# Keys spread two tiles ahead on GpSimd, and mask matmuls ahead of score matmuls

## The chip, the cores and the metric

The kernel runs on one core of a Trainium2 chip. Time is device time of the whole execution in microseconds (us), lower is better. Engines are named as in the profile: PE is TensorE's matmuls and PEld its weight loads, DVE is VectorE, ACT is ScalarE, POOL is GpSimd, SP is SyncE, which issues the DMAs.

## The reference, cut to what matters

There are 32 batches of a context `ctx` (128 channels by 1024 positions). Two things are computed from it and combined. The first is attention within chunks of 64 positions, with 8 heads of 16 channels and one bias for masked keys:

```
scores = einsum('bnqhd,bnkhd->bnhqk', qh, kh) * scale
scores = scores + where(mask > 0, 0.0, -1e9)
out    = softmax(scores) @ v, projected, masked, plus x, then normalised over positions
```

The second is a nearest-neighbour search over each batch: pairwise distances of all 1024 positions, the 30 nearest of each position (`top_k(pd, 30)`), the differences of three coordinates to each neighbour, their length and two angles. Those go through batch norms, give weights, and the weighted sum of neighbours is added to the first part.

## The kernel before, in words

`stage_a` (lines 146 to 1160) does attention, the distances, the top 30, the gathering of the neighbours' coordinates and the angles. Stage B (about 4140 to 4340 us) sums batch-norm moments, stage E (to the end) applies the weights. Only stage A is touched.

A batch `b` has 8 tiles of 128 positions (`TILES`), in two halves of 4 (`QT`). Each engine has its own program, an instruction stream with waits on semaphores, and each runs the batches through `emit(b, j, par, first, last)`: four batches written out, a loop over pairs of batches, and two written out. Order within an engine is fixed by that program.

DVE takes the tiles in pairs (0,1), (2,3), (4,5), (6,7). For a pair it does four rounds `r` of MAX8, FIND_INDEX8 and (but for the last) MATCH_REPLACE8 on 1024 distances per row (lines 866 to 873). Behind rounds 0 and 2 it takes the reciprocal of a tile's softmax sums (`inverse`, L900) and the row maxima of a tile's scores (`largest`, L896). Behind round 2 of pair (2,3) and of pair (6,7) it splits the found indices of half a batch into digits (`digits`, L827, L831, L835). Behind round 1 of pair (6,7) it takes the reciprocal of the denominators of the angles of batch `b-2` (`denoms`, L891), which waits for POOL's `sph_denoms` of that batch.

PE, iteration `t`: units of the gather for batch `b-1` (a one-hot fill L482 and 12 short matmuls L503), the two halves of the distances of tile `t+2` (L407, L409, bank `pd_ps`), then `scores` of tile `t+1`, a unit, the transposes `turn_probs` of tile `t-1` (L453), a unit, `values` of tile `t-1` (L463), and by the iteration further projections (L568, L425, L416). The scores of a tile are one PSUM bank `s_ps` of 128 x 512: partitions 0 to 63 are the tile's first chunk (`e` = 0), partitions 64 to 127 its second. Each chunk's half is a bf16 mask matmul from 32 rows (L441), which starts the accumulation, and an f32 matmul of 128 rows (L444), which ends it. `scores` waits until ACT has taken the exponents of the tile before from the same bank (`exp_ready`), and until POOL has written this tile's keys (`kz_ready`).

ACT, iteration `t`: it empties the one-hot banks (L588 to `ohT`), the distance halves (L588 to `pd_sb`), takes the exponents of tile `t` between the two distance halves (L754), then empties what PE made.

POOL, iteration `t` (lines 1032 to 1087): `spread_keys` (L1115) multiplies the tile's keys with the head mask into `kz[:, t % 2]`, two buffers of 128 x 1024 f32, and waits until the scores two tiles before have been made. Behind it stands `normalise` of tile `t-1` (L1091), which waits for DVE's `inverse` and releases PE's `turn_probs`. Then come parts of the gather for the batch before (L958 to L965), and in some iterations long pieces: at `t` = 3 `sph_signs` of batch `b-2` (16 steps, L987 to L1003), at `t` = 4 `invert` and `squares_split` (L916 to L929), at `t` = 5 `sph_denoms` (L1011 to L1015).

Keys and queries of a half lie in `kt` and `qs`. PE makes those of the next half at the end of iterations 2 and 6 and ACT writes them; ACT's write of `kt` waits until all four tiles of the old half have been spread.

Of the kernel before, what the change touches and what calls it, by code (L numbers as in the profile page):

```python
# [25 lines left out]
HEADS, CHUNK = 8, 64  # L26
# [7 lines left out]
QT = TILES // QUADS  # L34
# [111 lines left out]
def stage_a(nc, x, ctx, mask, w_in, b_in, w_out, b_out, consts, y_dram, cst, con, planes, idx_all, stats_all):  # L146
    OHR = 3
    XR = 97
    with ExitStack() as st:
        def sb(name, shape, dt=F32):  # L150
            return st.enter_context(nc.sbuf_tensor(name, shape, dt))
# [40 lines left out]
        qs = sb("qs", [P, HALF])  # L192
        kt = sb("kt", [P, HALF])
        kz = sb("kz", [P, 2, 2, HEADS, CHUNK])
# [11 lines left out]
        s_ps = st.enter_context(nc.psum_tensor("s_ps", [P, HEADS, CHUNK], F32))  # L206
# [72 lines left out]
        def misc_base(b):  # L279

            return 5 if isinstance(b, int) and b == 0 else b * FILLS
# [8 lines left out]
        def batches(eng, emit):  # L290

            emit(0, 0, 0, True, False)
            emit(1, 0, 1, False, False)
            emit(2, 1, 0, False, False)
            emit(3, 1, 1, False, False)
            with eng.Fori(2, B // 2 - 1) as j:
                emit(j * 2, j, 0, False, False)
                emit(j * 2 + 1, j, 1, False, False)
            emit(B - 2, B // 2 - 1, 0, False, False)
            emit(B - 1, B // 2 - 1, 1, False, True)  # L300
# [60 lines left out]
        def _(pe):  # L361
            pe.wait_ge(w_in_landed, 96)
            for g in range(4):
                m = nc.tensor.transpose(mi_ps[0][:, g * C:(g + 1) * C], wnat[:, g, :], con["ident"])
# [64 lines left out]
            def scores(b, par, t):  # L429

                s = b * TILES + t

                if not (isinstance(s, int) and s == 0):
                    pe.wait_ge(exp_ready, s)
                pe.wait_ge(kz_ready, s + 1)
                if t == 0:
                    pe.wait_ge(minv_ready, b + 1)
                for e in range(2):
                    ch = 2 * (t % QT) + e
                    keys = minv[:, par, (2 * t + e) * CHUNK:(2 * t + e + 1) * CHUNK]  # L440
                    nc.tensor.matmul(s_ps[64 * e:64 * e + 64], negs[MASKS],  # L441
                                     keys.rearrange("p (o k) -> p o k", o=1).to_broadcast([32, HEADS, CHUNK]),
                                     start=True, stop=False)
                    m = nc.tensor.matmul(s_ps[64 * e:64 * e + 64], qs[:, bass.ts(ch, CHUNK)], kz[:, t % 2, e],  # L444
                                         start=False, stop=True)
                m.then_inc(s_ready, 1)

# [462 lines left out]
        def _(pool):  # L910
# [121 lines left out]
            def emit(b, j, par, first, last):  # L1032
                second = isinstance(b, int) and b == 1
                steps = Steps((b - 1) * GSTEPS - (0 if first or second else len(slot_groups[0]) * 4))
                for t in range(TILES):
                    h = t // QT
                    s = b * TILES + t

                    if t % QT != QT - 1:
                        spread_keys(b, t + 1)  # L1040

                    if t == QT - 1:
                        pool.wait_ge(misc_moved, misc_base(b) + (8 if first else 12))
                        spread_keys(b, t + 1)
                    elif t == TILES - 1 and not last:
                        pool.wait_ge(misc_moved, misc_base(b) + (24 if first else 29))
                        spread_keys(b + 1, 0)
                    if t > 0 or not first:
                        normalise(s - 1, (t - 1) % TILES)
                    if t == QT + 1:  # L1050
                        rows(b, j, par, 0, misc_base(b) + (15 if first else 20))
                    elif t == 1 and not first:
                        rows(b - 1, (b - 1) // 2 if isinstance(b, int) else (j - 1 if par == 0 else j), 1 - par, 1, misc_base(b) + 4)
                    if t == 0 and not first:
                        keep(b - 1, 1 - par)
                    if t == 3 and not first:
                        convert(b - 1, 1)
                    if t == 7:
                        convert(b, 0)
                    if t > 0 and not first:  # L1060
                        gather(b - 1, 1 - par, 0 if t <= QT else 1, slot_groups[t % QT], steps)
                    elif t == 0 and not first and not second:
                        gather(b - 2, par, QUADS - 1, slot_groups[0], steps)
                    if t == 0 and there(b - 3):
                        sph_ratios(b - 3)
                    if t == 3:
                        if there(b - 3):
                            sph_turn(b - 3)
                        if there(b - 2):
                            sph_signs(b - 2)  # L1070
                    if t == 5 and there(b - 2):
                        sph_denoms(b - 2)
                    if t == 2:
                        split(b, j, par)
                    if t == 1 and not last:
                        square(b + 1, (b + 1) // 2 if isinstance(b, int) else (j if par == 0 else j + 1), 1 - par)
                    if t == 4 and not last:
                        if first:
                            gate(pool, probs_ready, s, pool_gates)
                        else:  # L1080
                            gate(pool, g_done, (b - 1) * NG + GROUPS, pool_gates)
                        invert(b + 1, (b + 1) // 2 if isinstance(b, int) else (j if par == 0 else j + 1), 1 - par)
                        squares_split(b + 1, 1 - par, misc_base(b) + (12 if first else 16))
                    if t == 5 and not first:
                        gate(pool, mv_ready, b, pool_gates)
                        nc.gpsimd.tensor_copy(stats_all[:, bass.ds(b - 1, 1), :].rearrange("p b s -> p (b s)"),
                                              mv[:]).then_inc(mv_kept, 1)

            def normalise(s, t):
                pool.wait_ge(rcp_ready, s + 1)  # L1090
                nc.gpsimd.tensor_tensor(sS[:, t % 2], sS[:, t % 2],  # L1091
                                        rs[:, t % 2, :].rearrange("p (h o) -> p h o", o=1).to_broadcast([P, HEADS, CHUNK]),
                                        ALU.mult).then_inc(probs_ready, 1)

            def rows(b, j, par, h, moved):

                pool.wait_ge(misc_moved, moved)
                if h == 0:
                    pool.wait_ge(mask_landed[par], (j + 1) * 16)
                    pool.wait_ge(x_landed, b * 16 + 16)  # L1100
                cols = bass.ts(h, HALF)
                nc.gpsimd.tensor_tensor(y_s[:, h, :], y_s[:, h, :], maskb[:, par, cols], ALU.mult).then_inc(masked_y, 1)
                pool.wait_ge(masked_y, b * 2 + h + 1)
                nc.gpsimd.tensor_tensor(y_s[:, h, :], y_s[:, h, :], x_s[:, cols], ALU.add).then_inc(y_ready, 1)

            def spread_keys(b, t):

                s = b * TILES + t

                if not (isinstance(s, int) and s < 2):  # L1110
                    pool.wait_ge(s_ready, s - 1)
                c = t % QT
                src = kt[:, 2 * c * CHUNK:2 * (c + 1) * CHUNK].rearrange("p (e o k) -> p e o k", e=2, o=1)
                heads = con["headmask"].rearrange("p (o h u) -> p o h u", o=1, u=1)
                nc.gpsimd.tensor_tensor(kz[:, t % 2], src.to_broadcast([P, 2, HEADS, CHUNK]),  # L1115
                                        heads.to_broadcast([P, 2, HEADS, CHUNK]), ALU.mult).then_inc(kz_ready, 1)
# [12 lines left out]
            def keep(b, par):  # L1129

                gate(pool, topk_done, (b + 1) * TILES, pool_gates)
                for q in range(QUADS):
                    dst = idx_all[:, bass.ds(b * BCOLS + q * QCOLS, QCOLS)].rearrange("p (k t) -> p k t", t=QT)
                    nc.gpsimd.tensor_copy(dst, idx16[:, par, q * QT:(q + 1) * QT, 0:K].rearrange("p t k -> p k t")).then_inc(idx_kept, 1)
# [4 lines left out]
            squares_split(0, 0, 2)  # L1139
            pool.wait_ge(misc_moved, 5)  # L1140
            spread_keys(0, 0)
            batches(pool, emit)
            normalise(B * TILES - 1, TILES - 1)
            rows(B - 1, B // 2 - 1, 1, 1, TAIL + 3)
# [874 lines left out]
```

## Time and profile before

| | |
|---|---|
| median of 3 runs | 5825.07 us (5822.19 to 5827.9) |
| the profiled execution's own time | 5831.42 us |
| its span | 5829.4 us |
| PE busy, share of the span | 4784.7 us, 82% |
| DVE busy | 5153.9 us, 88% |
| ACT busy | 4027.0 us, 69% |
| POOL busy | 3047.6 us, 52% |
| mean granted TensorE clock | 0.908 |

Stage A ends near 4140 us of the span. A batch takes about 126 us there. A busy share over the whole span mixes the stages; POOL works only in stage A. Distances between starts on PE tell more than its busy times, since its matmuls are pipelined.

### The profile page before, as it was taken

What the parts mean: (1) busy time and instruction counts of PE and PEld (TensorE: products, weight loads), DVE (VectorE), ACT (ScalarE), POOL (GpSimd) and SP (SyncE); (2) the same over time, 40 slices, a digit from 0 to 9 for tenths busy, and PEclk for the clock granted to TensorE, in tenths of its full rate; (3) what the DMA queues carried; (4) which work ended last, traced back from release to release, by engine and by line L of the source; (5) the groups of instructions that cost most, each with busy time, mean ns of one, the idle gap of its engine ahead of it and who ended that gap; (6) DMA issues with size and microseconds to landing.
All of it is one profiled execution on the core that took longest, in us unless ns stands there. A gap on an engine that the chain in (4) does not pass through costs nothing. (4 is left out here: it accounts for less than half of the span.)

```text
span 5829.4 us, 169462 instructions
## 1 busy us (share of the span) xinstructions
PE 4784.7 (82%) x63182; PEld 2694.6 (46%) x63182; DVE 5153.9 (88%) x7549; ACT 4027.0 (69%) x9505; POOL 3047.6 (52%) x3780
## 2 busy tenths in 40 slices
PE   6888878888888888888888888887395889899999
PEld 2444444444444444444444444443242666666666
DVE  7999989999999999998999999898298988888887
ACT  3777777777777777777777777776533766666666
POOL 3577777777777777777777777776400000000000
PEclk8999999899898999989999998898697899999999
DMA  0010000010000001000000100000000000000000
GB/s 29 16 31 16 16 17 16 17 31 17 17 16 17 17 16 31 16 17 16 17 17 16 31 16 17 16 16 12 1 0 4 26 27 30 32 26 30 26 30 26
DMA packets 135798, 114.60 MB, mean 20 GB/s; under 512 B 105344, under 2 KB 106112, under 8 KB 134784
## 3 DMA queue, kind: packets, MB, share of 16 engines
q1 hardware_dynamic: 134912, 102.73, 6.0%
q8 instruction: 563, 9.22, 0.7%
q14 instruction: 323, 2.65, 0.2%
HBM read 69.16 MB, written 33.55 MB: 18 GB/s over the span
## 5 line engine op out<-in xcount | busy, mean ns | idle before, releaser
L588 ACT ACTIVATE ohT<-oh_ps 128x512 bf16<-128x512 f32 x1920 | 1149.0, 613 | 564.8 <-PE oh_ps L482 560.4
L866 DVE MAX8 vals<-pd_sb 128x8 f32<-128x1024 f32 x1024 | 1201.0, 1210 | 310.8 <-ACT pd_sb L588 293.4
L871 DVE FIND_INDEX8 idx<-vals,pd_sb 128x8 uint16<-128x1024 f32 x1024 | 1243.6, 1217 | 0.0
L503 PEld LDWEIGHTS g_ps<-tparts,ohT 128*128 128x128 bf16 x23040 | 851.5, 97 | 347.5 <-issue 103.1
L482 PE MATMUL oh_ps<-bitsT,code 128*128 128x512 bf16 x1920 | 777.8, 411 | 284.9 <-ACT bitsT L772 154.0
L873 DVE MATCH_REPLACE8 pd_sb<-vals,pd_sb 128x1024 f32<-128x1024 f32 x768 | 927.5, 1208 | 0.0
L503 PE MATMUL g_ps<-tparts,ohT 128*128 128x24 bf16 x23040 | 869.3, 174 | 3.3
L1955 PEld LDWEIGHTS e_a_ps<-planes,e_oh 120*128 120x128 bf16 x24576 | 687.2, 97 | 301.9 <-issue 220.7
L1725 ACT COPY e_at<-e_a_ps 128x512 f32<-128x512 f32 x512 | 543.0, 1061 | 358.5 <-PE e_a_ps L1955 353.6
L1955 PE MATMUL e_a_ps<-planes,e_oh 120*128 120x32 bf16 x24576 | 702.1, 178 | 87.6 <-DVE e_oh L1883 46.8
L407 PE MATMUL pd_ps<-ctx_s 128*128 128x512 f32 x1024 | 661.7, 732 | 75.4 <-ACT pd_sb L588 73.6
L444 PE MATMUL s_ps<-kz,qs 128*64 128x512 f32 x1024 | 639.5, 710 | 0.0
L754 ACT ACTIVATE sS<-s_ps,mx 128x64 f32<-128x64 f32 x2048 | 610.7, 329 | 29.8 <-DVE mx L896 28.5
L1883 DVE TENSOR_TENSOR e_oh<-e_pairs,e_iotan 120x2048 bf16<-120x2048 bf16 x512 | 622.2, 1216 | 5.0 <-PE e_a_ps L1955 2.2
L1115 POOL TENSOR_TENSOR kz<-kt,cst 128x1024 f32<-128x1024 f32 x256 | 490.0, 1914 | 242.3 <-ACT kt L588 185.1
L961 POOL TENSOR_TENSOR gsb<-gsb 128x240 f32<-128x240 f32 (+2 forms) x1152 | 544.6, 473 | 90.3
L482 PEld LDWEIGHTS oh_ps<-bitsT,code 128*128 128x128 bf16 x1920 | 187.8, 101 | 850.7 <-issue 443.6
L1969 PE MATMUL e_o_ps<-e_at,e_xT 128*128 128x512 f32 x1024 | 566.6, 648 | 0.2 <-ACT e_at L1725 0.2
L588 ACT ACTIVATE pd_sb<-pd_ps,nxx 128x512 f32<-128x512 f32 x512 | 366.5, 716 | 200.4 <-PE pd_ps L409 200.4
L1091 POOL TENSOR_TENSOR sS<-sS,rs 128x512 f32<-128x512 f32 x256 | 273.2, 1067 | 402.2 <-DVE rs L900 402.1
L754 ACT ACTIVATION_READ_ACCUMULATOR sS<-s_ps,mx 128x1 f32 x2048 | 455.7, 223 | 0.0
L441 PE MATMUL s_ps<-xp,negs 32*64 32x512 bf16 x512 | 221.0, 432 | 278.0 <-ACT sS L754 157.1
(241 smaller groups left out, 7430.5 us busy)
## 6 DMA issues: line engine op xcount, KB each, us to landing
ctx_s<-in_ctx SPq DMA_DIRECT2D x32, 512.0 KB, 4.4
maskb<-in_mask_Bx1x_ff SPq DMA_DIRECT2D x32, 512.0 KB, 6.6
x_s<-in_x SPq DMA_DIRECT2D x32, 512.0 KB, 5.1
y_spill<-y_s SPq DMA_DIRECT2D x32, 512.0 KB, 3.0
e_y<-y_spill SPq DMA_DIRECT2D x32, 512.0 KB, 3.9
out<-e_o SPq DMA_DIRECT2D x64, 256.0 KB, 2.2
table<-in_ctx SPq DMA_DIRECT2D x96, 4.0 KB, 5.8
pd_sb<-in_shape_constants SPq DMA_DIRECT2D x1, 1180.0 KB, 5.3
```

Source lines behind the costliest of these rows:

```text
L407: nc.tensor.matmul(pd_ps[:], ctx_s[:, par, bass.ts(t, P)], ctx_s[:, par, bass.ts(h, HALF)], start=True, stop=False)
L444: m = nc.tensor.matmul(s_ps[64 * e:64 * e + 64], qs[:, bass.ts(ch, CHUNK)], kz[:, t % 2, e], start=False, stop=True)
L482: nc.tensor.matmul(oh_ps[k % 2][:], code[:, k % KT, :], bitsT[:, k // KT, :], start=True, stop=True).then_inc(oh_ready, 1)
L503: m = nc.tensor.matmul(found_ps[gi % 2][:, k % GK, t, :], ohT[:, k % OHR, bass.ts(t, P)], tparts[:, par, part, :], start=(part == 0), stop ...
L588: return nc.scalar.activation(dst, src, func, scale=scale, bias=bias)
L754: m = nc.scalar.activation(sS[:, t % 2, hd, :], s_ps[:, hd, :], ACT.Exp, bias=mx[:, t % 2, hd:hd + 1], accum_out=rs[:, t % 2, hd:hd + 1])
L866: nc.vector.max(vals[:, i, :], pd_sb[:, (t + i) % RING, :]).then_inc(topk_step, 1)
L871: found = nc.vector.max_index(idx16[:, par, t + i, 8 * r:8 * r + 8], vals[:, i, :], work)
L873: nc.vector.match_replace(work, vals[:, i, :], work, REMOVED).then_inc(topk_step, 1)
L1883: v.tensor_tensor(oh[pp, g % RING], low.to_broadcast([QCOLS, NB // 2, LO, 2]), row.to_broadcast([QCOLS, NB // 2, LO, 2]), ALU.is_equal).th ...
L1955: m = nc.tensor.matmul(a_ps[g % 2][:, i].rearrange("p t e -> p (t e)"), oh[pp, g % RING, i // 2, :, i % 2], spr[q][pp, part, :, (g * NB + ...
L1969: m = nc.tensor.matmul(o_ps[q][:], xT[:, par, e, :], at[:, q, e].rearrange("p t n -> p (t n)"), start=(e == 0), stop=(e == HI - 1))
```

## The change

In `scores`, both mask matmuls of a tile are issued first and both score matmuls after them. In POOL's program the keys of tile `t+2` are spread in iterations 0, 1 of each half, none in iteration 2, and those of the next half's first two tiles together in iteration 3. One more spread stands ahead of the first batch. The number of matmuls and of spreads and their operands stay as they were. `spread_keys` itself is unchanged: its wait for the scores two tiles before the spread one stays.

```diff
@@ scores (PE) @@
                 for e in range(2):
-                    ch = 2 * (t % QT) + e
                     keys = minv[:, par, (2 * t + e) * CHUNK:(2 * t + e + 1) * CHUNK]
                     nc.tensor.matmul(s_ps[64 * e:64 * e + 64], negs[MASKS],
                                      keys.rearrange("p (o k) -> p o k", o=1).to_broadcast([32, HEADS, CHUNK]),
                                      start=True, stop=False)
-                    m = nc.tensor.matmul(s_ps[64 * e:64 * e + 64], qs[:, bass.ts(ch, CHUNK)], kz[:, t % 2, e],
+                for e in range(2):
+                    m = nc.tensor.matmul(s_ps[64 * e:64 * e + 64], qs[:, bass.ts(2 * (t % QT) + e, CHUNK)], kz[:, t % 2, e],
                                          start=False, stop=True)
                 m.then_inc(s_ready, 1)
@@ emit (POOL) @@
-                    if t % QT != QT - 1:
-                        spread_keys(b, t + 1)
-
-                    if t == QT - 1:
+                    if t % QT < 2:
+                        spread_keys(b, t + 2)
+                    elif t == QT - 1:
                         pool.wait_ge(misc_moved, misc_base(b) + (8 if first else 12))
                         spread_keys(b, t + 1)
+                        spread_keys(b, t + 2)
                     elif t == TILES - 1 and not last:
                         pool.wait_ge(misc_moved, misc_base(b) + (24 if first else 29))
                         spread_keys(b + 1, 0)
+                        spread_keys(b + 1, 1)
                     if t > 0 or not first:
                         normalise(s - 1, (t - 1) % TILES)
@@ ahead of the batches (POOL) @@
             spread_keys(0, 0)
+            spread_keys(0, 1)
             batches(pool, emit)
```

## Rows read from the trace of the kernel before

**Rows 1.** Waits, whole span: engine line waited for, us in total, times, longest.

```profile
ACT ohT L588 <- PE oh_ps L482: 560.4, 350, 6.2
DVE vals L866 <- ACT pd_sb L588: 293.4, 45, 21.7
```

**Rows 2.** Timeline of DVE in one batch: start, duration, then line, operation, idle before.

```profile
1960.98 1.12 DVE L827 TENSOR_TENSOR bits<-idx,bitval 128x896 uint16<-128x896 uint16 x1
...
2004.42 1.23 DVE L866 MAX8 vals<-pd_sb 128x8 f32<-128x1024 f32 x1 [7.51 <-ACT pd_sb L588]
...
2018.20 1.64 DVE L891 RECIPROCAL rel<-rel 128x240 f32<-128x240 f32 x1
...
2068.28 1.23 DVE L866 MAX8 vals<-pd_sb 128x8 f32<-128x1024 f32 x1 [4.69 <-ACT pd_sb L588]
```

**Rows 3.** Timeline of POOL from iteration 3 to iteration 5 of that batch.

```profile
1957.23 1.90 POOL L1115 TENSOR_TENSOR kz<-kt,cst 128x1024 f32<-128x1024 f32 x1 [2.50 <-ACT kt L588]
1960.59 1.04 POOL L1091 TENSOR_TENSOR sS<-sS,rs 128x512 f32<-128x512 f32 x1 [1.46 <-DVE rs L900]
...
1983.68 1.90 POOL L1115 TENSOR_TENSOR kz<-kt,cst 128x1024 f32<-128x1024 f32 x1 [0.25 <-POOL turn L1003]
1985.54 1.04 POOL L1091 TENSOR_TENSOR sS<-sS,rs 128x512 f32<-128x512 f32 x1
...
2005.37 1.04 POOL L1091 TENSOR_TENSOR sS<-sS,rs 128x512 f32<-128x512 f32 x1
...
2015.74 0.69 POOL L1015 TENSOR_TENSOR rel<-rel 128x240 f32<-128x240 f32 x1 [0.19 <-POOL planes L1014]
```

**Rows 4.** Timeline of PE, iterations 4 and 5 of that batch.

```profile
1985.72 0.37 PE L441 MATMUL s_ps<-xp,negs 32*64 32x512 bf16 x1 [2.42 <-POOL kz L1115]
...
1988.89 0.64 PE L453 MATMUL mi_ps<-cst,sS 128*128 128x128 f32 x4
...
2005.56 0.60 PE L441 MATMUL s_ps<-xp,negs 32*64 32x512 bf16 x1 [4.24 <-POOL kz L1115]
...
2011.22 1.09 PE L453 MATMUL mi_ps<-cst,sS 128*128 128x128 f32 x4
```

**Rows 5.** Windows (length, busy by engine, PEclk): the second of those score blocks.

```profile
2005.60:2010.50 4.90, 4.90 (x7) 0.80 (x8) 4.90 (x10) 0.00 (x0) 4.74 (x5) 0.50 0.00 0
```

**Rows 6.** Timeline of PE: a score block, and a block of 64-column f32 matmuls.

```profile
2052.93 0.40 PE L441 MATMUL s_ps<-xp,negs 32*64 32x512 bf16 x1 [0.52 <-ACT sS L754]
2053.26 1.07 PE L444 MATMUL s_ps<-kz,qs 128*64 128x512 f32 x2
...
2055.59 0.39 PE L482 MATMUL oh_ps<-bitsT,code 128*128 128x512 bf16 x1
...
2059.70 1.97 PE L425 MATMUL mi_ps<-wT,ctx_s 128*64 128x128 f32 x32
2061.61 0.39 PE L482 MATMUL oh_ps<-bitsT,code 128*128 128x512 bf16 x1
```

**Rows 7.** Timeline of POOL and DVE: last denominators of the first and last steady batch.

```profile
375.10 0.71 POOL L1015 TENSOR_TENSOR rel<-rel 128x240 f32<-128x240 f32 x1 [0.18 <-POOL planes L1014]
...
377.95 1.65 DVE L891 RECIPROCAL rel<-rel 128x240 f32<-128x240 f32 x1
...
3916.39 0.71 POOL L1015 TENSOR_TENSOR rel<-rel 128x240 f32<-128x240 f32 x1 [0.18 <-POOL planes L1014]
...
3920.37 1.64 DVE L891 RECIPROCAL rel<-rel 128x240 f32<-128x240 f32 x1
```

**Rows 8.** Timeline of DVE: the digits of pair (6,7) in two batches.

```profile
2027.39 0.61 DVE L827 TENSOR_TENSOR bits<-idx,bitval 128x896 uint16<-128x896 uint16 x1
...
2028.26 0.66 DVE L835 TENSOR_TENSOR hi1h<-hi,hival 128x960 bf16<-128x960 uint16 x1
...
2155.86 2.25 DVE L827 TENSOR_TENSOR bits<-idx,bitval 128x896 uint16<-128x896 uint16 x1
...
2159.20 1.26 DVE L835 TENSOR_TENSOR hi1h<-hi,hival 128x960 bf16<-128x960 uint16 x1
```

## The prediction

> **What bounds the kernel now.** The page's shares come first: DVE is busy 88% of the span, POOL half of it, and POOL works only in stage A. The view by waits then says what DVE lacks there: one line, 293.4 us in 45 waits for distances that ACT writes [rows 1]. DVE's timeline shows where. The wait recurs once in each batch, at MAX8 of tile 7 (7.51 us at 2004.42; 7.5 to 10.0 in others), and eight times more at tile 3 (from 923.0 to 3335.99 us, 17.7 us together, the largest 4.69) [rows 2]. Outside these, DVE is busy. So stage A is DVE's work plus some 8 us a batch, and the question is what makes tile 7 late.
>
> Backward from 2004.42: ACT writes tile 7's second distance half behind the exponents of tile 5, those stand behind roots and projections of iteration 4, these behind PE's transposes L453 at 1988.89, these behind the scores of tile 5, which began at 1985.72 after 2.42 us of waiting for `kz` [rows 4]. POOL wrote that `kz` only at 1983.68, behind `sph_signs` [rows 3]. [...]
>
> **The change, part by part.**
>
> Spreads. Tile 5 is now spread in iteration 3, before `sph_signs`, and tile 6 at the start of iteration 4, so both waits of PE for `kz` go. What is late next is `normalise`: in iteration 4 POOL still does one spread (tile 6) behind `sph_signs`, then `normalise(3)`, ending at 1985.54 + 1.04 = 1986.58. PE's transposes can start then instead of at 1988.89: 2.3 us gained [rows 3, 4]. In the same way iteration 5's transposes move from 2011.22 to 2005.37 + 1.04 = 2006.41, 4.8 us earlier [rows 3, 4].
>
> Does the second spread in iteration 3 delay POOL? It adds 1.90 us behind 1957.23 + 1.90; `normalise(2)` began at 1960.59 only after 1.46 us of waiting for DVE, so its start would move from 1960.59 to about 1961.0, and POOL waits for DVE's digits behind it anyway [rows 3]. Cost: nothing while keys come no later than now, up to 1.9 us a batch if they came just in time. They come earlier, see next. The new spread's wait (scores of tile 3) is long met, and the extra buffer it fills is free for the same reason.
>
> Matmul order. A score block takes 2055.59 - 2052.93 = 2.66 us, of which each f32 score takes about 1.0 (2.66 / 2 - 0.33) [rows 6]. Grouped, the two scores stand side by side, in different column halves. No row shows that pair. The nearest is L425: 32 passes of 128 x 128, alternating between column halves, in 2061.61 - 2059.70 = 1.91 us. [...] Bounds: nothing gained (2.66), both wholly side by side (1.3). I take 1.75, by the L425 row. Where it counts: ACT waits after each block for the next fill (560.4 us in 350 waits, 1.6 each), so 0.9 us a tile comes off the PE-ACT chain [rows 1]. Over iterations 0 to 3 that brings keys, and PE's arrival at iteration 4, some 3 us earlier, which covers the spread above.
>
> [...]
>
> What then binds. DVE's gain is not 8 us a batch. DVE's L891 in pair (6,7) waits for POOL's L1015. Here L1015 ended at 2015.74 + 0.69 = 2016.43, and L891 started at 2018.20: 1.77 us later [rows 2, 3]. Between DVE's digits (1960.98) and L1015 POOL runs almost without a gap, 55.5 us, and none of that work is removed or moved off. So the stretch can shrink by this slack alone. The 29 steady pairs, from 375.81/377.95 to 3917.10/3920.37, have slacks of 1.56 to 4.37, sum 69 us [rows 7]. The large ones are batches where PE came late to iteration 4, which the 0.9 per tile mends. Less 0.1 each for the semaphore: 66 us. Where PE now waits for `normalise(3)` for over 2 us its clock can fall to the lower level (as in rows 5); L453 took 1.09 there against 0.64 [rows 4]. I take 1.5 us of that on a third of the batches beyond what the chain's spare 0.6 hides: 8 us lost. 58 us stay.
>
> Tile 3's waits (17.7 us) go with the 4.8 us of iteration 5 [rows 2]. The start and last batches give about 5 more.
>
> Against it: in iteration 7 two spreads in a row meet DVE's digits of pair (6,7). These took from 2028.26 + 0.66 - 2027.39 = 1.53 us with POOL idle to 2159.20 + 1.26 - 2155.86 = 4.60 beside one spread and `normalise` [rows 8]; over the batches they average 3.5. DVE and POOL are now both locked to L1015's end: POOL reaches the pair of spreads about 7.9 us after it, DVE the digits 9.3 after it, so every batch collides, at about 4.6. That is 1.1 x 29 = 32 us lost; bounds from 1.53 (a gain of 57) to one whole spread more, 4.60 + 1.90 (87 lost). [...]
>
> Sum: 58 + 18 + 5 - 32 = 49 us off the profiled execution's 5831.4: 5782. It lies 6.4 above the median of runs, so the median would be 5776.
>
> **Rivals.**
>
> A: the score halves don't overlap. The waits for `kz` still go: PE's arrival in iteration 4 gains 1.3 us in the half of batches that waited for `kz`, the others nothing. About 20 + 18 + 3 - 32 = 9 us: 5816. [...] Chance 0.12.
>
> B: the collision in iteration 7 costs nothing more than now (keys or normalise fall elsewhere) and the clock holds: 66 + 18 + 5 = 89 us less, 5736, or some between. For it: the 1.53 row; against: both engines hang on L1015. Chance 0.15.
>
> [...] Chance 0.08.
>
> D: the change moves waits only, POOL comes later by the second spread (up to 1.9 x 29 = 55 us, eating the 49): 5830, no change. Chance 0.07.
>
> **How the numbers follow.** The forecast's case has 0.58, giving 5776, own range 5755 to 5800. The whole range, 5740 to 5818, takes in most of A and B. A measurement here tells 0.2% (12 us) from no change: faster means under 5813. Faster: 0.58 + 0.15 and a third of A, 0.78 rounded. Same: the rest of A and half of D, 0.12. Slower: C and part of D, 0.10.
>
> **What would show it.** In the profile after: L441's waits for POOL `kz`, as in rows 4, near nothing; start of the mask pair to the next fill 1.75 us at full clock; L453 of iteration 4 directly behind `normalise`; tile 7's wait down to 5 to 6 us; L891 starting within 0.2 us of L1015's end, at times waiting for it; tile 3's waits gone; digits of pair (6,7) near 4.6 in each batch. It is wrong if the block stays above 2.3 us, if L891 keeps its slack, or if tile 7's wait is gone altogether.

## The result, and the profile after

The changed kernel takes 5790.46 us (median of 5 runs, 5786.69 to 5792.12). The kernel before, on the same chip, takes 5822.19 (5 runs, 5817.2 to 5827.9). The ratio is 0.9939, with a 95% interval of [0.9927, 0.9951]: faster by 0.6%. The forecast was 5776, its own range 5755 to 5800. The profiled execution took 5790.79 against 5831.42 before, 40.6 us less; the prediction's sum said 49.

The page of the kernel after, its head, its busy row, and TensorE's granted clock in 40 slices:

```profile
span 5788.7 us, 168877 instructions
...
PE 4476.3 (77%) x62610; PEld 2718.6 (47%) x63182; DVE 5127.8 (89%) x7549; ACT 4035.6 (70%) x9505; POOL 3045.6 (53%) x3780
...
PEclk7888888888888898888888888887697899999999
```

DVE is still the engine that is nearly always busy, and its busy time fell by 26.1 us (5153.9 before) though it runs the same 7549 instructions. The waits of the kernel after (engine line waited for: total us, times, longest), against [rows 1] and the waits for `kz` in [rows 4]:

```profile
DVE vals L866 <- ACT pd_sb L588: 284.0, 35, 21.7
...
ACT ohT L588 <- PE oh_ps L482: 114.4, 245, 2.2
...
DVE rel L891 <- POOL rel L1015: 92.1, 2, 48.5
...
ACT gsb L669 <- POOL planes L965: 86.2, 88, 1.5
...
ACT sS L754 <- DVE mx L896: 168.1, 90, 5.2
...
PE mi_ps L453 <- POOL sS L1092: 66.4, 36, 5.4
```

PE now waits for `kz` only once, 2.8 us ahead of the first scores, and ACT's wait for PE's code planes fell from 560.4 to 114.4 (all idle time ahead of these copies: from 564.8 to 155.3; the trace lacks 572 of the 1920 records of L482 and so cannot name the cause of each wait). Both are what the change aims at, and almost none of it reached DVE: its wait for distances fell by 9.4 only. Two rows are new. ACT now waits 86.2 us in 88 places for POOL's L965, and PE's transposes wait for `normalise`. A third has grown: ACT waits 168.1 us for the row maxima that DVE makes of the scores, where it was 28.5. A good part of what PE and ACT save is time in which they now wait for DVE and POOL.

PE and POOL of the kernel after, at iteration 4 of one batch, against [rows 3, 4, 6] (start, duration, then what ran; in brackets the idle time before and what ended it):

```profile
1839.66 0.40 PE L440 MATMUL s_ps<-xp,negs 32*64 32x512 bf16 x2 [0.52 <-ACT sS L754]
1839.99 1.08 PE L444 MATMUL s_ps<-kz,qs 128*64 128x512 f32 x4
1841.00 0.10 PEld L482 LDWEIGHTS oh_ps<-bitsT,code 128*128 128x128 bf16 x1 [0.81 <-issue]
...
1841.19 1.90 POOL L1116 TENSOR_TENSOR kz<-kt,cst 128x1024 f32<-128x1024 f32 x1 [0.25 <-PE s_ps L444]
...
1843.05 1.04 POOL L1092 TENSOR_TENSOR sS<-sS,rs 128x512 f32<-128x512 f32 x1
...
1844.23 1.08 PE L453 MATMUL mi_ps<-cst,sS 128*128 128x128 f32 x4 [2.55 <-POOL sS L1092]
...
1847.43 0.56 ACT L669 COPY gsb<-g_ps 128x480 f32<-128x480 f32 x1 [0.99 <-POOL planes L965]
...
1848.31 2.07 PE L568 MATMUL mi_ps<-oT,wT 128*128 128x512 f32 x2 [0.81 <-ACT oT L588]
...
1850.31 3.37 PE L425 MATMUL mi_ps<-wT,ctx_s 128*64 128x128 f32 x32
```

The score block, from the masks to the next fill, takes 1841.00 - 1839.66 = 1.34 us; it was 2.66. Both are the medians of 248 blocks too. Four f32 passes of 512 columns now take 1.08 us together, as long as two of them took before [rows 6]: the halves run wholly side by side. L453 starts behind `normalise(3)`, as forecast. But PE stood idle for 2.55 us, and what follows is slow: L453 takes 1.08 (0.63 in other batches, as below), L425 3.37 (1.97 in [rows 6]). The windows of that stretch (length, busy time and count of PE, PEld, DVE, ACT and POOL, then the granted clock, the DMA share and GB/s):

```profile
1844.20:1853.60 9.40, 8.56 (x80) 6.01 (x80) 9.40 (x16) 3.82 (x8) 8.28 (x11) 0.52 0.01 3
1853.60:1863.00 9.40, 5.31 (x63) 2.89 (x64) 0.79 (x1) 9.14 (x28) 8.33 (x7) 1.00 0.01 2
```

For 9.4 us behind the idle stretch the granted clock is 0.52, and in the 9.4 us behind those it is 1.00. In 15 of 30 batches L453 is slow like this. In the others it runs at full rate after a wait that is mostly shorter, but the clock falls a little later. One of them, with the window in which it is low:

```profile
1968.99 0.63 PE L453 MATMUL mi_ps<-cst,sS 128*128 128x128 f32 x4 [1.28 <-POOL sS L1092]
...
1972.20 0.56 ACT L669 COPY gsb<-g_ps 128x480 f32<-128x480 f32 x1 [1.46 <-POOL planes L965]
...
1973.08 2.08 PE L568 MATMUL mi_ps<-oT,wT 128*128 128x512 f32 x2 [1.74 <-ACT oT L588]
1975.09 2.45 PE L425 MATMUL mi_ps<-wT,ctx_s 128*64 128x128 f32 x32
```

```profile
1972.70:1976.10 3.40, 3.02 (x12) 1.52 (x14) 3.40 (x7) 1.50 (x4) 2.69 (x6) 0.50 0.01 2
```

L568 takes 2.08 us here, behind 1.74 us in which PE stood idle. Only 4 of the 30 batches run L568 and L425 at the full rate, such as this one:

```profile
1597.82 1.12 PE L568 MATMUL mi_ps<-oT,wT 128*128 128x512 f32 x2 [0.86 <-ACT oT L588]
1598.88 2.03 PE L425 MATMUL mi_ps<-wT,ctx_s 128*64 128x128 f32 x32
...
1610.82 1.23 DVE L866 MAX8 vals<-pd_sb 128x8 f32<-128x1024 f32 x1 [6.92 <-ACT pd_sb L588]
```

Tile 7's MAX8 starts 13.0 us behind the start of L568 there, and 15.0 us on average in the other 26. In the kernel before all 30 ran L568 and L425 at the full rate, with the same 13.0 us, and PE idle for 0.18 us ahead of L568.

In both of the batches last shown ACT's copy of the gathered bank waits for POOL as well, 1.46 us in the first. The copy has two buffers, and the older is free only when POOL's gather is through with it. That gather stands behind this iteration's spread and `normalise(3)`.

DVE and POOL around pair (6,7), against [rows 7, 8]:

```profile
1863.61 1.23 DVE L866 MAX8 vals<-pd_sb 128x8 f32<-128x1024 f32 x1 [9.23 <-ACT pd_sb L588]
...
1873.22 0.70 POOL L1015 TENSOR_TENSOR rel<-rel 128x240 f32<-128x240 f32 x1 [0.19 <-POOL planes L1014]
...
1877.22 1.64 DVE L891 RECIPROCAL rel<-rel 128x240 f32<-128x240 f32 x1
...
1881.89 3.77 POOL L1116 TENSOR_TENSOR kz<-kt,cst 128x1024 f32<-128x1024 f32 x2
...
1886.02 1.04 POOL L1092 TENSOR_TENSOR sS<-sS,rs 128x512 f32<-128x512 f32 x1 [0.37 <-DVE rs L900]
1886.42 1.13 DVE L827 TENSOR_TENSOR bits<-idx,bitval 128x896 uint16<-128x896 uint16 x1
1887.47 0.29 DVE L831 TENSOR_SCALAR hi<-idx 128x120 uint16<-128x120 uint16 x1
1887.79 0.66 DVE L835 TENSOR_TENSOR hi1h<-hi,hival 128x960 bf16<-128x960 uint16 x1
```

Tile 7's wait is still there (9.23 here; mean over 30 batches 8.48, before 8.14, the first two batches left out in both), and L891 starts 1877.22 - 1873.92 = 3.3 us after L1015's end: the slack that the prediction meant to spend is kept (over the 29 steady pairs it sums to 79 us, before 69). So DVE reaches the digits when both spreads are over (1881.89 + 3.77 = 1885.66), and they cost 2.03 us here. Over all pairs, DVE's digit rows before and after (busy total, mean ns):

```profile
L835 DVE TENSOR_TENSOR hi1h<-hi,hival 128x960 bf16<-128x960 uint16 x64 | 60.5, 945 | 2.2
L831 DVE TENSOR_SCALAR hi<-idx 128x120 uint16<-128x120 uint16 x64 | 45.0, 703 | 0.0
```

```profile
L835 DVE TENSOR_TENSOR hi1h<-hi,hival 128x960 bf16<-128x960 uint16 x64 | 50.5, 790 | 2.2
L831 DVE TENSOR_SCALAR hi<-idx 128x120 uint16<-128x120 uint16 x64 | 30.4, 474 | 0.0
```

That is 24.6 of the 26.1 us. The small waits of DVE, at tile 3 (18.8, now 1.3) and at tile 7 of the first two batches, went from 22.0 to 2.5, while tile 7's in the other 30 grew by 10.2. Together 26.1 + 9.4 = 35.5 of the 40.7 us of span.

### The profile page after: what moved, and what is told of

Read it like the earlier page. It is cut to its first block and busy times, and to the rows that moved or that the text cites. A ratio compares the mean times of both kernels' runs of the same rounds, so it can differ in the third digit from the quotient of the medians.

```text
span 5788.7 us, 168877 instructions
## 1 busy us (share of the span) xinstructions
PE 4476.3 (77%) x62610; PEld 2718.6 (47%) x63182; DVE 5127.8 (89%) x7549; ACT 4035.6 (70%) x9505; POOL 3045.6 (53%) x3780
## 5 line engine op out<-in xcount | busy, mean ns | idle before, releaser
L866 DVE MAX8 vals<-pd_sb 128x8 f32<-128x1024 f32 x1024 | 1200.6, 1211 | 302.2 <-ACT pd_sb L588 284.0
L588 ACT ACTIVATE ohT<-oh_ps 128x512 bf16<-128x512 f32 x1920 | 1152.0, 615 | 155.3 <-PE oh_ps L482 114.4
L503 PEld LDWEIGHTS g_ps<-tparts,ohT 128*128 128x128 bf16 x23040 | 871.8, 99 | 380.9 <-issue 148.7
L503 PE MATMUL g_ps<-tparts,ohT 128*128 128x24 bf16 x23040 | 883.9, 175 | 81.6 <-issue 33.5
L482 PE MATMUL oh_ps<-bitsT,code 128*128 128x512 bf16 x1348 | 590.3, 442 | 293.4 <-ACT bitsT L772 155.7
L754 ACT ACTIVATE sS<-s_ps,mx 128x64 f32<-128x64 f32 x2048 | 611.5, 329 | 169.4 <-DVE mx L896 168.1
L482 PEld LDWEIGHTS oh_ps<-bitsT,code 128*128 128x128 bf16 x1920 | 192.8, 103 | 849.2 <-ACT ohT L588 360.8
L1116 POOL TENSOR_TENSOR kz<-kt,cst 128x1024 f32<-128x1024 f32 x256 | 484.3, 1902 | 172.2 <-ACT kt L588 101.0
L958 POOL TENSOR_TENSOR gsb<-gsb,hi1h 128x480 f32<-128x480 f32 x384 | 439.9, 1146 | 12.5 <-DVE hi1h L835 8.7
L440 PE MATMUL s_ps<-xp,negs 32*64 32x512 bf16 x512 | 110.2, 427 | 370.2 <-ACT sS L754 367.0
```

What stands on the lines that cost most here:

```text
L482: nc.tensor.matmul(oh_ps[k % 2][:], code[:, k % KT, :], bitsT[:, k // KT, :], start=True, stop=True).then_inc(oh_ready, 1)
L503: m = nc.tensor.matmul(found_ps[gi % 2][:, k % GK, t, :], ohT[:, k % OHR, bass.ts(t, P)], tparts[:, par, part, :], start=(part == 0), stop ...
L588: return nc.scalar.activation(dst, src, func, scale=scale, bias=bias)
L754: m = nc.scalar.activation(sS[:, t % 2, hd, :], s_ps[:, hd, :], ACT.Exp, bias=mx[:, t % 2, hd:hd + 1], accum_out=rs[:, t % 2, hd:hd + 1])
L866: nc.vector.max(vals[:, i, :], pd_sb[:, (t + i) % RING, :]).then_inc(topk_step, 1)
```

## The experiments

Each experiment ran beside the kernel before, not all on the same chip, and that kernel's median lay between 5826.3 and 5831.4 there. So kernels are best compared by their ratios to it.

One account serves all of them. DVE binds stage A, so a kernel's span should move by the sum of DVE's busy time, its wait at MAX8 (L866) for ACT and its wait at L891 for L1015. From the page and the waits of each profile, in us; the last two columns are differences from before, of that sum and of the span:

| kernel | DVE busy | MAX8 waits | L891 waits | sum | span |
|---|---|---|---|---|---|
| before | 5153.9 | 293.4 | 91.6 | 0 | 0 |
| after | 5127.8 | 284.0 | 92.1 | -35 | -41 |
| e1 order alone | 5157.2 | 254.6 | 91.8 | -35 | -36 |
| e2 spreads alone | 5197.1 | 259.9 | 91.6 | +10 | +9 |
| e3 PE kept busy | 5151.6 | 250.3 | 92.0 | -45 | -54 |
| e4 `normalise`, gather, spread | 5183.7 | 199.1 | 109.2 | -47 | -50 |
| e5 `normalise`, spread, gather | 5124.5 | 290.3 | 91.9 | -32 | -35 |
| e6 e4, second spread late | 5156.8 | 186.9 | 108.7 | -87 | -91 |
| e7 e6, reciprocal late | 5126.9 | 191.1 | 91.7 | -129 | -136 |
| e8 e7, iteration 3's late too | 5146.5 | 282.8 | 91.7 | -18 | -17 |
| e9 e7, old order | 5179.8 | 236.8 | 91.7 | -31 | -35 |
| e10 e7, iteration 5's late too | 5116.1 | 178.4 | 91.7 | -153 | -160 |
| e11 after, iteration 7's late | 5118.8 | 264.4 | 91.5 | -64 | -67 |

The sum holds within 9 us in every row. The span is DVE's busy time and all its idle time by definition, so what this shows is that its other waits hardly moved. It says where time went, not why. (91.6 of the L891 waits are 2 waits outside the steady batches. The row of e10 is of its fastest run.)

Why tile 7 is late is told by two things in iteration 4, read from every profile's timelines: when ACT's copy of the gathered bank (L669) starts, and whether PE runs L425, which follows L568, at the full rate (1.97 to 2.03 us) or slower (2.45 us or more). Times are means over 30 batches, in us behind the end of `sph_signs` (L1003):

| kernel | copy starts | L425 slow | tile 7's MAX8, L425 at full rate | the same, L425 slow | all |
|---|---|---|---|---|---|
| before | 7.81 | 0 of 30 | 21.70 | none | 21.70 |
| after | 6.47 | 26 | 20.33 | 22.33 | 22.06 |
| e3 | 6.46 | 14 | 20.31 | 21.87 | 21.04 |
| e4 | 4.69 | 14 | 18.49 | 20.54 | 19.44 |
| e5 | 6.41 | 29 | 20.20 | 22.30 | 22.23 |
| e7 | 4.57 | 10 | 18.45 | 20.13 | 19.01 |
| e8 | 4.55 | 23 | 18.42 | 20.35 | 19.90 |

At the full rate MAX8 follows the copy by 13.9 us in every row. In the batches with a slow L425 it starts 1.6 to 2.1 us later than in the others of its kernel. The granted clock in the first 1.2 us of those slow L425 lay between 0.50 and 0.72 in all six kernels that have them.

**e1: the matmul order alone.** The new order in the scores, with the spreads of the kernel before.

> The matmul order of the change alone, spreads as in the kernel before. My theory (the score block is halved to 1.33 us, but where PE then stands idle its clock falls and tile 7's wait stays): PE still waits for kz behind sph_signs, now for 3 us or more; block 1.33 at full clock, about 2.6 at the low one; tile 7's wait 8 to 9 us; tile 3's waits mostly gone; 5805 us. Rival (the order carries the whole gain of the change): 5790 us. Rival (the order is worth nothing without the spreads): 5822.

Measured 5797.46 us, ratio 0.9945 [0.9931, 0.9958]. The order alone is worth nearly the whole gain. PE arrives earlier and waits for `kz` instead:

```profile
PE s_ps L440 <- POOL kz L1115: 248.2, 89, 5.6
```

It was 120.9 in 56 waits before. Part of the time that PE saves is turned into this wait, yet MAX8's falls by 38.8: tile 3's 18.8 go, and tile 7's fall from 8.14 to 7.54 on average. DVE's busy time grows by 3.3.

**e2: the spreads alone.** The new spreads, with the interleaved order of before.

> The spreads of the change alone, mask and score matmuls interleaved as before. My theory: no wait of L441 for kz, block 2.66, PE comes to the transposes of tile 3 about 4.2 us behind sph_signs without standing idle, so at full clock; tile 7's wait 6.9 us where it was 7.5, unchanged where PE came late; tile 3's waits gone; 5800 us. Rival (the spreads carry the whole gain): 5790. Rival (the second spread in iteration 3 delays POOL, nothing won): 5822 or more.

Measured 5847.73 us, ratio 1.0033 [1.0021, 1.0044]: slower, against my 5800; the last rival was right. MAX8's waits fall by 33.5, as the waits for `kz` go, but DVE's busy time grows by 43.2. DVE's digit row beside the spreads:

```profile
L831 DVE TENSOR_SCALAR hi<-idx 128x120 uint16<-128x120 uint16 x64 | 67.0, 1047 | 0.0
```

And POOL's keys come no earlier (178.3 us of waiting for ACT's `kt`, 185.1 before, 101.0 after). So the second spread of iteration 3 delays POOL a little: from DVE's digits to the end of L1015 it needs 55.7 us in the median and at most 56.7, against 55.4 and 55.5 before. Most of the loss is in the digits themselves: those of pair (2,3) take 2.84 us on average, where it was 2.04, and those of pair (6,7) 4.12, where it was 3.48. The condition of the prediction, that keys come earlier, is what the order provides.

**e3: PE kept busy.** Does the low clock cost the gain?

```diff
                 ps = misc.open()
+                if t == QT - 1:
+                    for _ in range(8):
+                        nc.tensor.matmul(ps[:], code[:, 0, :], code[:, 0:4, :].rearrange("p a b -> p (a b)"),
+                                         start=True, stop=True)
```

> The changed kernel, with 8 bf16 matmuls of 128x512 (1.7 us at full clock) added on PE ahead of its wait for normalise(3); their result is overwritten by the transposes. My theory (the low clock behind that wait keeps tile 7 late): L453 of tile 3 at 0.63 in nearly every batch, where it is 1.08 in about half now, tile 7's wait falls from 8.7 to about 7.7 us on average, digits up by 0.5, 5776 us. Rival (the clock is not the cause; ACT or POOL holds tile 7 back anyway): wait and time stay, 5790, or 5800 by the added work.

Measured 5781.74 us, ratio 0.9922 [0.9908, 0.9935]. The transposes run at full rate in every batch (0.60 to 0.66), yet the whole is 9 us, 0.17%, better than after, and the two intervals overlap. Tile 7's wait is 6.2 to 6.9 in some batches and 8.2 to 8.5 in the others, mean 7.37. ACT waits for POOL's gather as in the kernel after, and somewhat more (103.1 us in 100 waits).

The filling does its work at L453 only. PE still stands idle ahead of L568, and behind that the clock falls in 14 of 30 batches (to 0.50 to 0.68 in the first 1.2 us of L425); these are the ones with the long wait. Two neighbouring batches, L572 being L568 here, the first with a granted clock of 0.58 from 1847.4 to 1851.5, the second with 1.00 from 1971.6 to 1975.0:

```profile
1847.49 2.01 PE L572 MATMUL mi_ps<-oT,wT 128*128 128x512 f32 x2 [1.78 <-ACT oT L592]
...
1862.05 1.23 DVE L870 MAX8 vals<-pd_sb 128x8 f32<-128x1024 f32 x1 [8.46 <-ACT pd_sb L592]
...
1971.63 1.13 PE L572 MATMUL mi_ps<-oT,wT 128*128 128x512 f32 x2 [1.80 <-ACT oT L592]
...
1984.61 1.23 DVE L870 MAX8 vals<-pd_sb 128x8 f32<-128x1024 f32 x1 [6.84 <-ACT pd_sb L592]
```

The copy starts at 6.46 as in after, so the 1.6 us between the two kinds of batches are the clock's. Why it falls in the one and not in the other, behind idle times of 1.78 and 1.80 us, is open. MAX8's waits fall by 33.7 us against after, and 23.8 come back in DVE's busy time, since DVE now meets the spreads with its digits (3.35 us on average in pair (6,7), 2.61 in after). The 9 us are therefore what is left of half of the effect, and not the price of the clock.

**e4: the spread behind `normalise` and gather.** Tile 6's spread leaves the head of iteration 4.

```diff
-                    if t % QT < 2:
+                    if t % QT < 2 and t != QT:
...
+                    if t == QT:
+                        spread_keys(b, t + 2)
+                        gate(pool, kz_ready, s + 3, pool_gates)
```

> The changed kernel, with POOL's spread of tile 6 moved behind normalise(3) and behind the gather of iteration 4 (one wait of POOL for its own spread is added). My theory: transposes of tile 3 at 1.4 us behind sph_signs instead of 3.3, PE idle for 0.7 us instead of 2.5, full clock; ACT's copy of the gathered bank no longer waits for POOL; tile 7's wait 5 to 6 us; L891 then starts within 0.2 us of L1015's end; digits of pair (6,7) near 4.4 instead of 2.6; 5760 us. Rival (tile 7's wait comes from iteration 5, table loads and exponents, whatever iteration 4 does): wait stays at 8.7, 5790 us.

Measured 5778.67 us, ratio 0.9914 [0.99, 0.9927]. I had said 5760. PE's transposes come 1.4 us behind `sph_signs` in most batches, instead of 3.3, and tile 7's wait falls to 5.73 on average (5.0 in many batches), what the prediction had expected of the change itself. I had expected ACT's copy to wait for POOL no more, and that did not come (111.9 us in all, 86.2 in after); but it starts 1.8 us earlier. The slack is closed: L891 waits. What the prediction said of the digits then comes true as well; DVE and POOL of e4, same batch as above:

```profile
1870.20 0.69 POOL L1015 TENSOR_TENSOR rel<-rel 128x240 f32<-128x240 f32 x1 [0.19 <-POOL planes L1014]
1870.93 1.65 DVE L891 RECIPROCAL rel<-rel 128x240 f32<-128x240 f32 x1 [1.23 <-POOL rel L1015]
...
1878.86 4.14 POOL L1119 TENSOR_TENSOR kz<-kt,cst 128x1024 f32<-128x1024 f32 x2
1880.14 1.11 DVE L827 TENSOR_TENSOR bits<-idx,bitval 128x896 uint16<-128x896 uint16 x1
1881.16 2.00 DVE L831 TENSOR_SCALAR hi<-idx 128x120 uint16<-128x120 uint16 x1
1883.19 1.32 DVE L835 TENSOR_TENSOR hi1h<-hi,hival 128x960 bf16<-128x960 uint16 x1
```

L831, 0.29 us alone, takes 2.00 and ends as POOL's pair of spreads ends (1883.0). The digits of pair (6,7) take 4.07 us on average (4.38 in many batches), 2.61 in after. Against the kernel before, 94 us of waiting came off MAX8; 30 went into DVE's busy time and 18 into L891.

**e5: `normalise`, spread, gather.** As e4, but the spread directly behind `normalise(3)`, ahead of the gather. PE gets its `normalise` early, ACT does not get its buffer. (POOL's added wait for its own spread, 0.4 us in e4, is left out here but in the first batch.)

> As e4, but tile 6's spread stands directly behind normalise(3), ahead of the gather of iteration 4. My theory (two things hold tile 7 in the changed kernel: the clock behind PE's idle wait, and ACT's copy of a gathered bank, which waits for POOL's gather): the transposes come at 1.4 us as in e4, but ACT still waits for POOL's gather until about 6.5 us behind sph_signs, so tile 7's wait is 6.5 to 7.5 us, between e4 (5.0) and the changed kernel (8.5); 5783 us. Rival (the clock alone): as e4, tile 7's wait 5.0, 5779 us.

Measured 5791.83 us, ratio 0.9932 [0.9919, 0.9946]: no better than after. My expectation for tile 7's wait was wrong; it is 8.64. PE and ACT of e5:

```profile
1843.40 0.63 PE L453 MATMUL mi_ps<-cst,sS 128*128 128x128 f32 x4 [0.24 <-POOL sS L1096]
...
1848.45 0.56 ACT L669 COPY gsb<-g_ps 128x480 f32<-128x480 f32 x1 [3.30 <-POOL planes L965]
...
1849.33 2.07 PE L568 MATMUL mi_ps<-oT,wT 128*128 128x512 f32 x2 [3.59 <-ACT oT L588]
```

The same two operations in e4, in a batch with a wait that is usual there:

```profile
2342.18 0.56 ACT L669 COPY gsb<-g_ps 128x480 f32<-128x480 f32 x1 [1.45 <-POOL planes L965]
...
2343.07 1.12 PE L568 MATMUL mi_ps<-oT,wT 128*128 128x512 f32 x2 [1.74 <-ACT oT L588]
```

What PE wins at L453 is lost at L669: ACT waits 2.98 us on average instead of 1.32, and the copy starts at 6.41 instead of 4.69. PE idles over 3 us behind it in most batches, and L568 or L425 is slow in 29 of 30, against 14 in e4. So an early `normalise` alone wins nothing. But e5 differs from e4 in two things, the copy and the clock. The batches at full rate part them: 18.49 us to tile 7's MAX8 in e4, 20.31 in e3, which has the late copy. The copy's place is worth 1.8 us, and the clock 1.6 to 2.1 us in each batch in which it falls. A third buffer for the copy would test it alone; it was not tried.

**e6: iteration 7's second spread late.** e4, and `spread_keys(b + 1, 1)` moved behind iteration 7's gather in the same way.

> e4 with the second spread of iteration 7 (tile 1 of the next batch) moved behind that iteration's gather. My theory (what DVE wins upstream is taken back where its digits of pair (6,7) meet two spreads in a row: the time from the end of L1015 to the end of the digits is what counts, 5.3 us beyond the 9.2 in the changed kernel, 4.4 in e4): digits 2.0 to 2.6 us instead of 4.38, L891 still waiting for L1015, 5730 us. Rival (the digits are slowed by whatever POOL does then, normalise and gather too): digits about 4, 5775 us.

Measured 5735.26 us, ratio 0.9834 [0.9821, 0.9848]. The time is as expected, the digits are not: 3.15 us on average (3.47 in many batches), since L891 still waits and so DVE still arrives at the remaining spread. One of two colliding spreads is gone (27 us of DVE's busy time).

**e7: the reciprocal late.** e6, and DVE's reciprocal goes behind the digits, so that DVE no longer waits for L1015 in this pair.

```diff
-                        if t == 6 and r == 1 and there(b - 2):
-                            denoms(b - 2)
...
                             digits(b, par, 0)
                             row_stats(b, 0)
+                            if there(b - 2):
+                                denoms(b - 2)
```

> e6 with DVE's reciprocal of the denominators moved behind the digits of pair (6,7), so that it no longer waits for L1015. My theory (in e4 and e6 POOL's chain binds DVE there, 1.22 us a batch): these 1.2 us go, tile 7's wait of 5 us stays or grows little, 5695 us. Rival (POOL binds the batch through normalise and kz as well, so the wait only moves to tile 7 or to the digits): 5730, as e6.

Measured 5695.41 us, ratio 0.978 [0.9766, 0.9795]: by its median the best of the kernels here, 95 us under after. The waits at L891 and the digits' excess both go (17.0 us, and 29.9 of DVE's busy time, against e6).

**e8: iteration 3's second spread late too.** e7 with `if t in (QT - 1, QT)` for the late spread.

> e7 with the second spread of iteration 3 behind its gather too, ahead of sph_signs. My theory: normalise(2) and the digits' conversion come a little earlier or as now, sph_signs starts up to 1.9 us later (the spread now stands in POOL's gapless stretch instead of in its waits), tile 7's wait grows by up to 1.9 us, 5700 to 5750 us. Rival (the waits in iteration 3 hide nothing): same as e7.

Measured 5814.33 us, ratio 0.9974 [0.9961, 0.9988], a miss by over 60 us. L453 is at 1.09 in 14 of 30 batches again and tile 7's wait at 8.52 on average. It is not the copy, which starts where it did in e7. The clock falls in 23 batches instead of 10 (0.50 to 0.71 in the first 1.2 us of their L425), which brings tile 7's distances 0.9 us later behind `sph_signs`. And POOL itself comes 2.1 us later: from DVE's digits to the end of L1015 it needs 57.5 us in the median, in e7 55.5.

**e9: e7 with the old order.**

> e7 with mask and score matmuls interleaved again as in the kernel before. My theory (the order of the matmuls takes 1.3 us off the PE-ACT chain of each tile, which counts where POOL does not hold PE): block 2.66 us, keys and the transposes later, tile 7's wait 1.3 us longer or more, tile 3's waits back; about 2 us a batch, 5760 us. Rival (with POOL's order mended the chain has room, and the order of the matmuls is worth nothing): 5695.

Measured 5793.88 us, ratio 0.9935 [0.9921, 0.9949]. I had said 5760: the order is worth more than that. By the ratios it is 1.55% or some 90 us to e7, and 0.55% or some 32 us to the kernel before (e1): it gives more where POOL is out of its way. What else e7 changes gives 0.65% without it, as this run shows.

**e10: iteration 5's spread late too.** e7 with `if t < 2` ahead and `if t in (QT, QT + 1)` behind.

> e7 with tile 7's spread in iteration 5 also moved behind normalise(4) and the gather. My theory (tile 7's distances are made ahead of that point, so it cannot shorten tile 7's wait; it only brings PE's transposes of tile 4 1.9 us earlier, where PE has room): within 10 us of e7, 5695. Rival (iteration 5's normalise is what the next batch waits for): 5670 or less.

Measured 5738.22 us, ratio 0.9862 [0.9847, 0.9877], but the five runs lie between 5671.49 and 5756.1, and the profiled one is the fastest. The median is 43 us above e7's, where I had said within 10. The account explains the profiled one (-153 against -160). Why the runs scatter so is open, and so is whether this spread's place gains or loses.

**e11: only iteration 7's second spread late.** The kernel after, with e6's last edit alone.

> The changed kernel with only the second spread of iteration 7 moved behind that iteration's gather. My theory (digits meet one spread less; but in the changed kernel they come late, when the pair is mostly over, and cost 2.6): digits 2.0 us, tile 7's wait unchanged at 8.5; 0.6 us a batch, 5775 us. Rival (the collision was never a cost in the changed kernel): 5790.

Measured 5764.53 us, ratio 0.9893 [0.9878, 0.9908]: 26 us under after. The digits of pair (6,7) go to 2.07 us, as expected, and MAX8's waits fall by 19.6 too, which I had not expected: tile 7's wait is 7.90 on average.

## Why the prediction was right, and where it was not

The sign and the size hold: 5790 in a range of 5755 to 5800. But the sum reached it by two large terms of which neither happened: 58 us gained at tile 7, where its wait grew, and 32 us lost in the digits, where 24 were gained. That their errors nearly cancel is luck. By one of the signs that the prediction gave itself ("if L891 keeps its slack") its mechanism is wrong.

- **Step 1, the waits for `kz`:** right. They are gone, and L453 stands directly behind `normalise(3)`.
- **Step 2, the second spread of iteration 3 costs nothing if keys come earlier:** right, with its condition; e2 takes the condition away and pays.
- **Step 3, the score block:** the two scores run side by side, as it said, and the term was mis-sized: 1.75 taken, 1.34 measured, at my lower bound of 1.3. The 1.75 was my estimate by the L425 row, and no run shows it: the block takes 1.34 in the median of 248, and the four f32 passes in it 1.08 together. That also refutes rival A. No run shows the 0.1 us taken off for each semaphore either; L891 starts 0.04 us behind L1015 in the batch shown of e4, where it waits.
- **Step 4, "tile 7's wait down to 5 to 6 us; L891 starting within 0.2 us of L1015's end" (58 us):** this step failed. The wait is 8.48 and L891 keeps 3.3 us in the batch shown. The prediction followed the chain only through PE, and made `normalise` what is late next. It missed that ACT's copy stands in the same chain and waits for POOL's gather, behind the same spread and `normalise`. So where the clock stays up, tile 7's distances come 1.4 us earlier behind `sph_signs` than before (20.33 against 21.70), not 2.3 and more. e4 moves the copy forward and the wait is 5.73; e5 leaves it and the wait is 8.64.
- **The clock (8 us of this step):** this term was far too small. The prediction looked at L453 alone, where the clock is low in half of the batches; on the way from L568 to tile 7's distances it is low in 26 of 30 (0.50 to 0.72 in the first 1.2 us of L425), behind PE's idle waits for `normalise` and for ACT. That takes 1.7 us a batch (22.06 against 20.33), some 52 us of lateness over 30 batches, and more than all that the copy left to be gained. What it would cost in time was not measured: e3 mends half of the batches and wins 9 us, since DVE's digits then meet the spreads.
- **Rival C, slower, the clock falls in every batch:** it nearly came on PE, with the low clock in 26 of 30 batches, and the wait at tile 7 grew by 0.34. That the kernel is faster all the same comes from the digits, which fell from 3.48 to 2.61 us, and from tile 3.
- **Rival B, the collision costs no more and the clock holds:** the first half came, the second did not.
- **Step 5, tile 3's waits:** right; 17.5 us less, where 18 was said. (There were 11 such waits before, 18.8 us; the prediction counted eight.)
- **Step 6, digits at 4.6 us in each batch (32 us lost):** wrong in sign here, since it hangs on step 4. With the slack kept, DVE arrives after the spreads, and the digits fell from 3.48 to 2.61 us: 24 us gained over all pairs. With the slack closed, e4 shows it nearly as forecast, 4.07 us on average. In the batch shown there L831 took 2.00 us, where it is 0.29 alone, and ended with the spreads; what makes it wait is not shown.
- **Rival D, waits are only moved:** nearest to what happened on PE and ACT. ACT's wait for code planes fell by 400 us and more, but all its idle time by 49 only (5829.4 - 4027.0 before, 5788.7 - 4035.6 after), and DVE's wait for distances by 9.4. What it lacked was the gain in the digits.

Taken by parts: the order alone gives 36 us of span, the spreads alone lose 9, both give 41. What the spreads add to the order (0.06% by the ratios) is not clear of noise. Added to the order, the spreads move 29.4 us out of DVE's busy time and the same 29.4 into its wait.

## What to carry to other kernels

Before a wait is counted as gained, list every engine that the chain passes through to the one that binds, with the buffer that each of them needs, and see who frees it: here the copy's buffer hung on the very queue that had been made longer. A PE that is made faster and then waits can fall to a lower clock, as here (0.52 granted for 9.4 us behind 2.55 us of idle time); read the rate of all that it runs on the chain behind the wait, not only of the first operation. Where one engine's work takes longer beside another's, as DVE's digits of pair (6,7) beside POOL's spreads (4.07 us on average in e4, 2.07 in e11), the same work has two prices, according to when it falls; a step that moves an engine's arrival moves this price too, and the two terms must be forecast together. Time taken out of one engine's wait shows in the total only in the binding engine's busy time plus its waits; keep that account for each version.

## What was not expected of the hardware

- Two f32 matmuls of 128 x 64 on 512 columns, in different column halves and with all rows in use, ran wholly side by side when one followed the other directly: 1.08 us for both, 1.07 for one of them when masks of another shape stood between [rows 6].
- A DVE instruction on uint16 of 0.29 us took 2.00 us beside a POOL spread, and another of 0.66 took 1.32 beside `normalise` (e4).
- After an idle stretch of 2.55 us on PE the granted clock was 0.52 for 9.4 us. With 1.28 us of waiting at the same place it stayed up for the matmuls just behind, and was 0.50 a little later, where PE had been idle for another 1.74 us.
- In the kernel before, where PE arrived late and hardly waited there (0.18 us ahead of L568), L568 and L425 ran at the full rate in all 30 batches.
